# Start, decode and end of a masked-attention kernel on one core: an earlier first load, a split last load, a shorter decode, another order at the end

## The chip, the core and the metric

The kernel runs on one core of a Trainium2 chip, on its five engines: TensorE (PE, matmuls and transposes), VectorE (DVE), ScalarE (ACT), GpSimd (POOL, which issues the loads of the adjacency) and SyncE (SP, which issues the other transfers). The metric is device time in microseconds of one launch. A profiled execution gives the trace that is quoted; its span runs from the first to the last instruction.

## The reference

One layer of graph attention with 4,096 items x and 4,096 entities, followed by a normalisation. The inputs' adjacency is an int32 matrix of 4,096 x 4,096, with a few ones in a row.

```python
scores = (x @ W @ a1)[:, None] + (entity_embs @ W @ a2)[None, :]
e = jnp.where(scores > 0, scores, 0.2 * scores)
e = jnp.where(adj > 0, e, -9e15)
attention = jax.nn.softmax(e, axis=1)
h = attention @ entity_embs + x
x = layernorm(x + elu(h))
```

Write p for the items' scores and q for the entities'. Each weight of the softmax is an exponential of max(p + q, 0.2 (p + q)), where the adjacency has a one.

## The kernel before, in words

The 4,096 items stand in four groups (g) of 1,024 columns, the entities in 32 blocks (b) of 128. A step is one group and one block, 128 in all; two steps are a pair (j), 16 pairs a group. A chunk is four blocks of one group, 32 chunks in all; GpSimd loads each from the int32 adjacency into the bf16 tile `raw` (line 272), which has five buffers, so that load n waits until TensorE has turned chunk n - 5.

**Before the first group.** SyncE loads the weights, the entities (1 MB) and x (four loads). GpSimd waits for the weights (line 280) before its first load. VectorE makes q, p, the scale of the codes and the shift of the softmax (lines 403 to 482) in many small steps; TensorE sends some of them to all partitions.

**Per pair.** TensorE turns it (`turn_pair`, line 698: 16 transposes of 128 x 128 into a PSUM tile `pairs`, of which there are two). ScalarE or VectorE (`by_dve` says which) takes it out as the mask in bf16, scaled (`store_pair`, lines 321 and 523). TensorE adds it to a histogram of codes (`add_hist`, line 714), from which the highest q among an item's neighbours is found.

**Per group, between its histogram and its first step.** ScalarE copies the histogram (line 329), TensorE spreads it (line 729), VectorE decodes it in nine instructions (`decode`, lines 492 to 512) into `dcol`, a column by item: the shift minus the leaky score of p and the highest q. TensorE turns `dcol` into rows over all partitions (`make_row`, line 736) and ScalarE copies them out (`take_row`, line 351, `drow`). For group 0 all this stands between its last chunk and its first step; for the later groups it is laid into the steps of the group before (the constants `HIST_COPY_AT` = 23 to `DROW_AT` = 28 say at which step). In group 0's second half TensorE and ScalarE also make the eight rows of p (`p_row`, lines 673 and 310), one ahead of each pair from pair 8 on; `p_row(c)` on TensorE waits for ScalarE's copy of row c - 1.

**Per step.** VectorE takes the smaller of mask and `drow` for a pair (line 534, `xm`) and adds the larger of p and the bend of q (line 542, `wts`); ScalarE exponentiates (line 335); TensorE sums weighted entities into `acc[0]` (line 749) and the weights into `acc[1]` (line 752). TensorE's steps lag by three.

**The end of a group.** `take_acc` copies both sums on ScalarE, TensorE turns them (`turn_sums`, `turn_back`), and `finish` in eleven parts divides, adds x, applies the elu (its exponential on ScalarE), adds x again, and normalises (the squares on ScalarE, the power on GpSimd). For groups 0 to 2 the parts lie in the steps of the next group (`FINISH_AT`); group 3's stand alone at the end. SyncE stores the result.

The order on each engine is the order of the code; semaphores connect the engines, and an engine does nothing behind an instruction that waits.

Of the kernel before, what the change touches and what calls it, by code (L numbers as in the profile page):

```python
# [5 lines left out]
P = 128  # L6
N, M, F = 4096, 4096, 64
# [11 lines left out]
CHUNKS = STEPS // CHUNK  # L19
RAWS = 5  # L20
# [34 lines left out]
def attention_layernorm(nc, x, adj, ent_blocks, turned_in, weights_in, out):  # L55
# [19 lines left out]
    with ctx:  # L75
# [50 lines left out]
        qbase = sb("qbase", [P, 1], fp32)  # L126
        empty = sb("empty", [P, NT], fp32)
# [26 lines left out]
        adj_in = [sem(f"adj_in{i}") for i in range(RAWS)]  # L154
        x_in = sem("x_in")
# [37 lines left out]
        d_done = sem("d_done")  # L193
        row_mm = sem("row_mm")
# [5 lines left out]
        acc_free = sem("acc_free")  # L200
        turn_sums_mm = sem("turn_sums_mm")
# [44 lines left out]

        def mask_made(engine, j):

            engine.wait_ge(dve_mask_done if by_dve(j) else act_mask_done, sum(by_dve(k) == by_dve(j) for k in range(j + 1)))
# [16 lines left out]
        def _(pool):  # L266
            def load(n):

                g, c = divmod(n, NB // CHUNK)
                if n >= RAWS:  # L270
                    pool.wait_ge(pair_mm, (n - RAWS + 1) * CHUNK // 2)
                pool.dma_start(raw[:, n % RAWS, 0:SIZES[g], :],  # L272
                               rows(adj, g)[:, :, P * CHUNK * c:P * CHUNK * (c + 1)]).then_inc(adj_in[n % RAWS], 16)
# [6 lines left out]
            pool.wait_ge(w_in, 16)  # L280
# [23 lines left out]
        def _(act):  # L304
# [7 lines left out]
            def store_pair(j):  # L312

                i = 2 * j
                if by_dve(j):
                    return
# [4 lines left out]
                act.activation(mask[:, i % RING:i % RING + 2, 0:n], pairs[j % 2][:, :, 0:n], ACT.Relu,  # L321
# [50 lines left out]
            take_row(0)  # L372
# [19 lines left out]
            squares(NG - 1)  # L392

        @block.vector
        def _(dve):
# [26 lines left out]
            def q_scale():  # L422
# [25 lines left out]
                dve.wait_ge(q_step, 6)  # L448
                dve.tensor_scalar(place[:, :], qcol[:, :], qmin_neg[:, :], qinv[:, :], ALU.add, ALU.mult).then_inc(q_step, 1)
# [24 lines left out]
            def find_shift():  # L474
# [7 lines left out]
                dve.tensor_scalar(q_bias[:, :], qcol[:, :], shift[:, :], None, ALU.subtract).then_inc(bias_done, 1)  # L482

            def decode(g):
# [3 lines left out]
                n = 7 * g  # L488
# [12 lines left out]
                dve.tensor_scalar(empty[:, s], st[:, 3, 0:m], 1.0, None, ALU.is_le)  # L501
# [349 lines left out]
```

## Time and profile before

| | |
|---|---|
| median of 3 runs | 354.25 us (353.78 to 355.08) |
| profiled execution | 353.8 us, its span 351.7 us |
| busy in the span | TensorE 80%, VectorE 84%, ScalarE 72%, GpSimd 12% |
| last landing of group 0 used | 52.96 us |
| first mask product (line 534) | 64.29 us |
| last copy out of `acc` begins | 336.91 us |
| last instruction on VectorE begins | 348.60 us |

Three stretches differ. Up to 53 us the engines work between landings of the adjacency; from there to 64 us one chain runs through four engines for group 0's decode; then the steps run to 336 us, and a last chain ends the span. The shares of busy time are means over all of them.

### The profile page before, as it was taken

The numbers are of one execution on the slowest core, as the hardware profiler recorded it, in microseconds if no ns is written. First come the engines' busy times: TensorE is split into PE (matmuls) and PEld (weight loads), VectorE is DVE, ScalarE is ACT, GpSimd is POOL, SyncE is SP. The second block draws the span as 40 slices with busy tenths as digits, with TensorE's granted clock in tenths as the row PEclk, the third lists the DMA queues.
The fourth block names the chain that finished last, engine by engine and source line by source line (L and its number), as shares of the span: only waits on it lengthen the run. The fifth ranks groups of instructions, "written<-read, shape, count | busy, mean of one in ns | idle before, by whom it ended". The sixth has DMA issues, their size and how long they took to land.

```text
span 351.7 us, 7943 instructions
## 1 busy us (share of the span) xinstructions
PE 280.9 (80%) x3470; PEld 142.3 (40%) x3470; DVE 296.7 (84%) x356; ACT 253.6 (72%) x216; POOL 40.9 (12%) x45
## 2 busy tenths in 40 slices
PE   1249675779999989999999999999959696667730
PEld 1146454535445544455445445545423232212210
DVE  1780523799988989999999999999999999999944
ACT  1087563399888949999999899999837764646620
POOL 6011110001101000000000310000040000002201
PEclk9998999699999999999999999999999999999985
DMA  7999999999999968887989591000000000000000
GB/s 149 257 207 208 207 207 207 207 208 206 207 175 187 151 101 126 136 131 120 152 140 145 85 173 32 2 3 2 2 0 32 3 0 2 0 2 0 32 0 30
DMA packets 34817, 37.23 MB, mean 106 GB/s; under 512 B 672, under 2 KB 33504, under 8 KB 34784
## 3 DMA queue, kind: packets, MB, share of 16 engines
q0 software_dynamic: 33280, 33.56, 59.0%
q1 hardware_dynamic: 1504, 3.18, 3.2%
q8 instruction: 27, 0.44, 0.5%
q14 instruction: 6, 0.05, 0.0%
HBM read 69.24 MB, written 1.05 MB: 200 GB/s over the span
## 4 chain that ended last, share of the span: by engine, by line
PE 32%; issue 22%; DVE 21%; DMA 13%; ACT 9%; POOL 2%; POOLq 1%; DVEq 0%; ACTq 0%
PE acc L749 12%; DMA raw<-adj_dram 12%; DVE xm L534 10%; PE pairs L698 10%; PE acc L752 6%; DVE wts L542 5%; ACT mask L321 5%; ACT wts L335 3%; PE hist L714 3%; POOL rstd L278 1%; DVE mask L523 1%; PE misc L729 1%; DMA w_sb<-weights_in_dram 1%; ACT drow L351 1%; POOL raw L272 1%
## 5 line engine op out<-in xcount | busy, mean ns | idle before, releaser
L335 ACT ACTIVATE wts<-wts,q_bias 128x1024 f32<-128x1024 f32 x128 | 143.5, 1150 | 45.1 <-DVE wts L542 44.4
L542 DVE SCALAR_TENSOR_TENSOR wts<-pb,q_bend,xm 128x1024 f32<-128x1024 f32 x128 | 160.5, 1279 | 2.0 <-PE acc L752 1.8
L749 PE MATMUL acc<-wts,ent_sb 128*32 128x512 f32 x1024 | 135.4, 601 | 16.8 <-ACT wts L335 13.1
L321 ACT ACTIVATE mask<-pairs 128x2048 bf16<-128x2048 bf16 x53 | 99.0, 1875 | 28.9 <-PE pairs L698 28.9
L698 PE MATMUL pairs<-ident,raw 128*128 128x128 bf16 x1024 | 71.3, 226 | 13.2 <-DMA raw<-adj_dram 10.3
L534 DVE TENSOR_TENSOR xm<-mask,drow 128x2048 bf16<-128x2048 bf16 x64 | 78.1, 1220 | 2.3 <-ACT drow L351 2.3
L752 PE MATMUL acc<-wts,onesf 128*32 128x256 f32 x1024 | 78.6, 379 | 0.0
L698 PEld LDWEIGHTS pairs<-ident,raw 128*128 128x128 bf16 x1024 | 61.6, 102 | 34.3 <-issue 23.0
L752 PEld LDWEIGHTS acc<-wts,onesf 128*32 128x32 f32 x1024 | 33.1, 111 | 77.6 <-issue 77.6
L272 POOL DMA_DIRECT2D raw<-adj_dram x32 | 28.3, 884 | 173.6 <-PE pairs L698 170.9
L749 PEld LDWEIGHTS acc<-wts,ent_sb 128*32 128x32 f32 x1024 | 26.7, 109 | 42.0 <-ACT wts L335 27.9
L523 DVE TENSOR_SCALAR mask<-pairs 128x2048 bf16<-128x2048 bf16 x11 | 13.5, 1223 | 17.1 <-PE pairs L698 17.1
L278 POOL TENSOR_TENSOR rstd<-var,mhalf 128x8 f32<-128x8 f32 x4 | 11.4, 2859 | 133.5 <-DVE var L612 133.4
L714 PE MATMUL hist<-mask,codes 128*32 128x512 bf16 x256 | 25.6, 395 | 0.8 <-DVE mask L523 0.8
L736 PE MATMUL misc<-ident,dcol 128*128 128x128 bf16 x32 | 3.3, 266 | 8.6 <-DVE dcol L512 8.6
L714 PEld LDWEIGHTS hist<-mask,codes 128*32 128x32 bf16 x256 | 7.0, 96 | 6.9 <-DVE mask L523 1.1
L659 PE MATMUL misc<-identf,qm 128*2 128x128 f32 x2 | 0.6, 394 | 9.6 <-DVE qm L419 9.6
L351 ACT ACTIVATE drow<-misc 128x1024 bf16<-128x1024 bf16 x4 | 4.0, 1010 | 4.9 <-PE misc L736 4.9
L472 DVE TENSOR_REDUCE p_all<-misc 1x1 f32<-1x128 f32 x1 | 0.3, 279 | 8.2 <-PE misc L678 8.2
L736 PEld LDWEIGHTS misc<-ident,dcol 128*128 128x128 bf16 x32 | 2.4, 119 | 10.2 <-DVE dcol L512 10.2
L575 DVE SCALAR_TENSOR_TENSOR y<-ent_sum,empty,misc 128x64 f32<-128x64 f32 x32 | 6.5, 274 | 0.1
L310 ACT ACTIVATE pb<-misc 128x512 f32<-128x512 f32 x8 | 4.8, 595 | 2.4 <-PE misc L673 2.4
(98 smaller groups left out, 101.2 us busy)
## 6 DMA issues: line engine op xcount, KB each, us to landing
raw<-adj_dram POOLq DMA_DIRECT2D x32, 1024.0 KB, 10.5
ent_sb<-ent_blocks_dram SPq DMA_DIRECT2D x1, 1024.0 KB, 7.5
x_sb<-x_dram SPq DMA_DIRECT2D x4, 256.0 KB, 8.6
out_dram<-y SPq DMA_DIRECT2D x4, 256.0 KB, 2.0
w_sb<-weights_in_dram SPq DMA_DIRECT2D x1, 32.5 KB, 2.1
```

The lines of the kernel that those rows point to most:

```text
L272: pool.dma_start(raw[:, n % RAWS, 0:SIZES[g], :], rows(adj, g)[:, :, P * CHUNK * c:P * CHUNK * (c + 1)]).then_inc(adj_in[n % RAWS], 16)
L278: pool.tensor_tensor(rstd[:, 0:n], var[:, 0:n], mhalf[:, 0:n], ALU.pow).then_inc(rstd_done, 1)
L321: act.activation(mask[:, i % RING:i % RING + 2, 0:n], pairs[j % 2][:, :, 0:n], ACT.Relu, scale=2.0 ** LIFT).then_inc(act_mask_done, 1)
L335: act.activation(part, part, ACT.Exp, bias=q_bias[:, b:b + 1]).then_inc(w_done, 1)
L351: act.activation(drow[:, g % 2, 0:cols(g)], row_ps[:, 0:cols(g)], ACT.Copy).then_inc(drow_done, 1)
L523: dve.tensor_scalar(mask[:, i % RING:i % RING + 2, 0:n], pairs[j % 2][:, :, 0:n], 2.0 ** LIFT, 0.0, ALU.mult, ALU.max).then_inc(dve_mask_d ...
L534: dve.tensor_tensor(xm[:, i % XS:i % XS + 2, 0:n], mask[:, i % RING:i % RING + 2, 0:n], drow[:, g % 2, 0:n].unsqueeze(1).to_broadcast([P, ...
L542: dve.scalar_tensor_tensor(wts[:, i % SLOTS, 0:n], pb[:, P * TILE0[g]:P * TILE0[g] + n], q_bend[:, b:b + 1], xm[:, i % XS, 0:n], ALU.max, ...
L698: ins = pe.transpose(pairs[j % 2][:, k, P * t:P * t + P], raw[:, n % RAWS, t, at:at + P], ident[:, :])
L714: ins = pe.matmul(hist[to:to + Q, 0:n], codes[:, i % NB, :], mask[:, i % RING, n * c:n * c + n], start=(pair == 0), stop=(pair == GROUP_PA ...
L749: pe.matmul(acc[0][to:to + Q, 0:n], ent_sb[:, b, Q * f:Q * f + Q], part[:, n * k:n * k + n], start=(b == 0), stop=(b == NB - 1))
L752: ins = pe.matmul(acc[1][Q * k:Q * k + Q, 0:P * m], onesf[:, 0:Q], part[:, P * t:P * t + P * m], start=(b == 0), stop=(b == NB - 1))
```

## The change

1. GpSimd's first load no longer waits for the weights.
2. Chunk 7, the last of group 0 (`LATE`), is loaded as two halves, the second with a semaphore of its own (`late_in`), for which only the last pair of the group waits. That pair's mask is shared: ScalarE takes its first block, VectorE its second; who needs the mask waits for both.
3. The decode has six instructions. Two slopes (`key_slope`) and two bases (`p_base`, `key_base`) are made once in `q_scale` and `find_shift`; the leaky score is then the smaller of two straight lines. `empty` comes last and has a semaphore, for which the totals wait. Group 0's rows are copied out by VectorE.
4. At the end, VectorE copies the last sums of weights while ScalarE copies the features; max(y, 0) + x has a place of its own (in a buffer of `wts`) and no longer waits for the exponential; VectorE squares.

```diff
-            pool.wait_ge(w_in, 16)
             load(0)
@@ load(n)
+                first = CHUNK // 2 if n == LATE else CHUNK
+                pool.dma_start(raw[:, n % RAWS, 0:SIZES[g], 0:P * first],
+                               rows(adj, g)[:, :, P * CHUNK * c:P * (CHUNK * c + first)]).then_inc(adj_in[n % RAWS], 16)
+                if n == LATE:
+                    pool.dma_start(raw[:, n % RAWS, 0:SIZES[g], P * first:P * CHUNK],
+                                   rows(adj, g)[:, :, P * (CHUNK * c + first):P * CHUNK * (c + 1)]).then_inc(late_in, 16)
@@ turn_pair(j)
                 pe.wait_ge(adj_in[n % RAWS], 16 * (n // RAWS + 1))
+                if j == GROUP_PAIRS - 1:
+                    pe.wait_ge(late_in, 16)
@@ who makes a mask
+        def by_act(j):
+            return j == GROUP_PAIRS - 1 or not by_dve(j)
@@ store_pair(j) on ScalarE
+                k = 1 if by_dve(j) else 2
+                act.activation(mask[:, i % RING:i % RING + k, 0:n], pairs[j % 2][:, 0:k, 0:n], ACT.Relu,
...
@@ decode(g), after the reduction
-                dve.tensor_scalar(empty[:, s], st[:, 3, 0:m], 1.0, None, ALU.is_le)
-                dve.tensor_scalar(st[:, 0, 0:m], st[:, 3, 0:m], qstep[:, :], qbase[:, :], ALU.mult, ALU.add).then_inc(st_step, 1)
-                dve.wait_ge(st_step, n + 4)
-                dve.tensor_tensor(st[:, 1, 0:m], st[:, 0, 0:m], pcol[:, s], ALU.add).then_inc(st_step, 1)
+                dve.scalar_tensor_tensor(st[:, 0, 0:m], st[:, 3, 0:m], key_slope[:, 0:1], p_base[:, s], ALU.mult,
+                                         ALU.add).then_inc(st_step, 1)
+                dve.tensor_scalar(st[:, 1, 0:m], st[:, 3, 0:m], key_slope[:, 1:2], key_base[:, :], ALU.mult,
+                                  ALU.add).then_inc(st_step, 1)
                 dve.wait_ge(st_step, n + 5)
-                dve.tensor_scalar(st[:, 2, 0:m], st[:, 1, 0:m], 0.0, 1 - ALPHA, ALU.max, ALU.mult).then_inc(st_step, 1)
-                dve.wait_ge(st_step, n + 6)
-                dve.scalar_tensor_tensor(st[:, 2, 0:m], st[:, 0, 0:m], ALPHA, st[:, 2, 0:m], ALU.mult, ALU.add).then_inc(st_step, 1)
-                dve.wait_ge(st_step, n + 7)
...
-                dve.tensor_scalar(dcol[:, 0:m], st[:, 2, 0:m], -1.0, shift[:, :], ALU.mult, ALU.add).then_inc(d_done, 1)
+                dve.tensor_tensor(dcol[:, 0:m], st[:, 0, 0:m], st[:, 1, 0:m], ALU.min).then_inc(d_done, 1)
+                dve.tensor_scalar(empty[:, s], st[:, 3, 0:m], 1.0, None, ALU.is_le).then_inc(empty_done, 1)
+
+            def take_row(g):
+                dve.wait_ge(row_mm, g + 1)
+                dve.tensor_copy(drow[:, g % 2, 0:cols(g)], row_ps[:, 0:cols(g)]).then_inc(drow_done, 1)
@@ the end, on VectorE (instead of the eleven parts in a row)
+                dve.wait_ge(w_used, STEPS)
...
+                dve.tensor_copy(wsum_sb[0:sums, 0:P * fourth(g)], acc[1][0:sums, 0:P * fourth(g)]).then_inc(last_wsum, 1)
+                for part in range(4):
+                    finish(g, part)
+                dve.wait_ge(att_done, NG)
+                fin_inc(dve.scalar_tensor_tensor(pos, y_g, 0.0, x_gr, ALU.max, ALU.add))
+                fin_wait()
+                dve.wait_ge(elu_done, NG)
+                fin_inc(dve.scalar_tensor_tensor(y_g, e_g, 1.0, pos, ALU.min, ALU.add))
+                for part in (6, 7):
+                    finish(g, part)
+                dve.wait_ge(centred, NG)
+                dve.tensor_tensor(e_g, y_g, y_g, ALU.mult).then_inc(square_done, 1)
+                for part in (8, 9, 10):
+                    finish(g, part)
```

GpSimd's program from its start on, before:

```order
L272 DMA raw<-adj_dram 128x8x512 [waits w_in]
L282 ISA
L282 IOTA steps_k 128x32
L284 MEMSET ident 128x128
L285 MEMSET identf 128x128
L287 AFFINE_SELECT identf<-identf 128x128 [waits ident_done]
L289 AFFINE_SELECT ident<-ident 128x128
L272 DMA raw<-adj_dram 128x8x512 x4
L272 DMA raw<-adj_dram 128x8x512 [waits pair_mm] x26
```

The same place on GpSimd in the changed kernel:

```order
L288 DMA raw<-adj_dram 128x8x512
L300 ISA
L300 IOTA steps_k 128x32
L302 MEMSET ident 128x128
L303 MEMSET identf 128x128
L305 AFFINE_SELECT identf<-identf 128x128 [waits ident_done]
L307 AFFINE_SELECT ident<-ident 128x128
L288 DMA raw<-adj_dram 128x8x512 x4
L288 DMA raw<-adj_dram 128x8x512 [waits pair_mm] x2
L288 DMA raw<-adj_dram 128x8x256 [waits pair_mm]
L291 DMA raw<-adj_dram 128x8x256
L288 DMA raw<-adj_dram 128x8x512 [waits pair_mm] x23
```

The first load has lost its wait; what stands behind it moves up with it, and the eighth load is now two of half the width.

VectorE at the end of group 0 before, from its own masks of that group (line 523) to the first mask product (line 534):

```order
L523 TENSOR_SCALAR mask<-pairs 128x2048 [waits pair_mm] x4
L492 SCALAR_TENSOR_TENSOR above<-misc,steps_key 128x256 [waits spread_mm]
L495 SCALAR_TENSOR_TENSOR above<-misc,above 128x256 [waits st_step]
L498 TENSOR_REDUCE st<-above 128x4x2 [waits st_step]
L501 TENSOR_SCALAR empty<-st 128x8 [waits st_step]
L502 TENSOR_SCALAR st<-st,qstep,qbase 128x8
L504 TENSOR_TENSOR st<-st,pcol 128x8 [waits st_step]
L506 TENSOR_SCALAR st<-st 128x8 [waits st_step]
L508 SCALAR_TENSOR_TENSOR st<-st 128x8 [waits st_step]
L512 TENSOR_SCALAR dcol<-st,shift 128x8 [waits st_step]
L534 TENSOR_TENSOR xm<-mask,drow 128x2048 [waits drow_done,act_mask_done,p_rows]
```

The same place on VectorE in the changed kernel:

```order
L553 TENSOR_SCALAR mask<-pairs 128x2048 [waits pair_mm] x3
L553 TENSOR_SCALAR mask<-pairs 128x1024 [waits pair_mm]
L518 SCALAR_TENSOR_TENSOR above<-misc,steps_key 128x256 [waits spread_mm]
L521 SCALAR_TENSOR_TENSOR above<-misc,above 128x256 [waits st_step]
L524 TENSOR_REDUCE st<-above 128x4x2 [waits st_step]
L529 SCALAR_TENSOR_TENSOR st<-st,key_slope,p_base 128x8 [waits shift_step,st_step]
L531 TENSOR_SCALAR st<-st,key_slope,key_base 128x8
L536 TENSOR_TENSOR dcol<-st 128x8 [waits st_step]
L537 TENSOR_SCALAR empty<-st 128x8
L541 COPY drow<-misc 128x1024 [waits row_mm]
L564 TENSOR_TENSOR xm<-mask,drow 128x2048 [waits drow_done,act_mask_done,p_rows]
```

The fourth mask is half as wide, the three steps that each waited for the one ahead have gone, `empty` stands behind `dcol`, and the copy of the rows has come over from ScalarE.

VectorE in the tail before, from the totals (line 560) to the variance (line 609):

```order
L560 SCALAR_TENSOR_TENSOR total<-empty,hist 128x8 [waits turn_sums_mm]
L565 RECIPROCAL total<-total 128x8 [waits sums_taken]
L575 SCALAR_TENSOR_TENSOR y<-ent_sum,empty,misc 128x64 [waits out_done,sum_done,turn_back_mm]
L590 TENSOR_TENSOR y<-y,total 128x512 [waits fin_step,feats_taken]
L593 TENSOR_TENSOR y<-y,x_sb 128x512 [waits fin_step]
L597 SCALAR_TENSOR_TENSOR y<-y,x_sb 128x512 [waits elu_done,att_done]
L600 SCALAR_TENSOR_TENSOR y<-e,y 128x512 [waits fin_step]
L603 TENSOR_REDUCE mean<-y 128x8 [waits fin_step]
L606 SCALAR_TENSOR_TENSOR y<-mean,y 128x512 [waits fin_step]
L609 TENSOR_REDUCE var<-e 128x8 [waits square_done]
```

The same place on VectorE in the changed kernel:

```order
L658 COPY wsum_sb<-acc 128x256 [waits turn_sums_mm,w_used]
L591 SCALAR_TENSOR_TENSOR total<-empty,hist 128x8 [waits empty_done,turn_sums_mm]
L596 RECIPROCAL total<-total 128x8 [waits sums_taken]
L606 SCALAR_TENSOR_TENSOR y<-ent_sum,empty,misc 128x64 [waits out_done,sum_done,turn_back_mm]
L621 TENSOR_TENSOR y<-y,total 128x512 [waits fin_step,feats_taken]
L624 TENSOR_TENSOR y<-y,x_sb 128x512 [waits fin_step]
L662 SCALAR_TENSOR_TENSOR wts<-y,x_sb 128x512 [waits att_done]
L665 SCALAR_TENSOR_TENSOR y<-e,wts 128x512 [waits elu_done,fin_step]
L634 TENSOR_REDUCE mean<-y 128x8 [waits fin_step]
L637 SCALAR_TENSOR_TENSOR y<-mean,y 128x512 [waits fin_step]
L669 TENSOR_TENSOR e<-y 128x512 [waits centred]
L640 TENSOR_REDUCE var<-e 128x8 [waits square_done]
```

A copy and the squares have come to VectorE, and the wait for the exponential stands one instruction later.

## Rows read from the trace of the kernel before

**Rows 1.** The chain that ended last, in order of time: start us, us, what.

```profile
31.22 21.70 DMA raw<-adj_dram
```

**Rows 2.** Waits of TensorE's line 698 up to 60 us: releaser, us, times.

```profile
  DMA raw<-adj_dram: 10.3, 8
```

**Rows 3.** Stretches: us, busy us of engines (instructions), clock, DMA share, GB/s.

```profile
70.00:160.00 90.00, 86.50 (x1144) 44.53 (x1148) 84.65 (x83) 79.63 (x65) 10.52 (x12) 1.00 1.02 164
210.00:330.00 120.00, 99.86 (x1188) 41.14 (x1188) 118.76 (x135) 88.18 (x80) 7.50 (x2) 0.99 0.04 8
```

**Rows 4.** DMA queues, 3.5 to 7 us: packets, MB, share of 16 engines.

```profile
q1 hardware_dynamic: 202, 0.83, 102.2%
```

**Rows 5.** DMA queues, 10 to 15 us.

```profile
q0 software_dynamic: 495, 0.51, 59.4%
q1 hardware_dynamic: 493, 0.91, 54.7%
```

**Rows 6.** DMA queues, 16 to 53 us.

```profile
q0 software_dynamic: 7570, 7.64, 124.0%
```

**Rows 7.** Timeline, 3 to 9 us: start us, us, instruction [idle before it, releaser].

```profile
3.13 1.03 POOL L272 DMA_DIRECT2D raw<-adj_dram  x1 [2.68 <-DMA w_sb<-weights_in_dram]
...
4.62 0.29 DVE L406 COPY wa_row<-acc 128x128 f32<-128x128 f32 x1 [1.27 <-PE acc L653]
...
8.93 2.29 DVE L411 TENSOR_TENSOR wts<-ent_sb,wa_row 128x2048 f32<-128x2048 f32 x1 [4.02 <-DMA ent_sb<-ent_blocks_dram]
```

**Rows 8.** Timeline, 47.5 to 58 us, the end of group 0.

```profile
51.51 0.62 PE L673 MATMUL misc<-identf,pcol 128*128 128x128 f32 x4 [0.41 <-ACT pb L310]
52.17 0.60 ACT L310 ACTIVATE pb<-misc 128x512 f32<-128x512 f32 x1 [0.80 <-PE misc L673]
...
52.96 1.07 PE L698 MATMUL pairs<-ident,raw 128*128 128x128 bf16 x16 [0.83 <-DMA raw<-adj_dram]
...
54.06 1.88 ACT L321 ACTIVATE mask<-pairs 128x2048 bf16<-128x2048 bf16 x1 [1.30 <-PE pairs L698]
...
55.87 1.23 DVE L523 TENSOR_SCALAR mask<-pairs 128x2048 bf16<-128x2048 bf16 x1 [3.84 <-PE pairs L698]
...
57.15 0.40 PE L714 MATMUL hist<-mask,codes 128*32 128x512 bf16 x4 [0.76 <-DVE mask L523]
```

**Rows 9.** Timeline, 126 to 130 us, group 1's decode.

```profile
126.92 0.42 DVE L498 TENSOR_REDUCE st<-above 128x8 f32<-128x256 f32 x1
...
127.37 0.17 DVE L501 TENSOR_SCALAR empty<-st 128x8 f32<-128x8 f32 x1
127.45 0.28 DVE L502 TENSOR_SCALAR st<-st,qstep,qbase 128x8 f32<-128x8 f32 x1
...
128.38 0.23 DVE L512 TENSOR_SCALAR dcol<-st,shift 128x8 bf16<-128x8 f32 x1
128.52 2.47 DVE L542 SCALAR_TENSOR_TENSOR wts<-pb,q_bend,xm 128x1024 f32<-128x1024 f32 x2
...
128.67 0.62 PE L736 MATMUL misc<-ident,dcol 128*128 128x128 bf16 x8 [0.91 <-DVE dcol L512]
```

**Rows 10.** Timeline, 62 to 66 us, group 0's rows.

```profile
63.14 1.02 ACT L351 ACTIVATE drow<-misc 128x1024 bf16<-128x1024 bf16 x1 [4.94 <-PE misc L736]
...
64.29 1.22 DVE L534 TENSOR_TENSOR xm<-mask,drow 128x2048 bf16<-128x2048 bf16 x1 [2.29 <-ACT drow L351]
```

**Rows 11.** Timeline, 315 to 352 us, the tail.

```profile
336.91 0.38 ACT L360 ACTIVATE wsum_sb<-acc 128x256 f32<-128x256 f32 x1
...
337.34 0.61 PE L767 MATMUL hist<-identf,wsum_sb 128*128 128x4 f32 x4 [0.99 <-ACT wsum_sb L360]
...
341.59 0.63 ACT L340 ACTIVATE e<-y 128x512 f32<-128x512 f32 x1 [4.30 <-DVE y L593]
...
342.32 0.69 DVE L597 SCALAR_TENSOR_TENSOR y<-y,x_sb 128x512 f32<-128x512 f32 x1 [0.77 <-ACT e L340]
343.05 0.69 DVE L600 SCALAR_TENSOR_TENSOR y<-e,y 128x512 f32<-128x512 f32 x1
```

More of the change, by code:

```diff
@@ L126, in attention_layernorm @@
         qbase = sb("qbase", [P, 1], fp32)
+        key_slope = sb("key_slope", [P, 2], fp32)
+        key_base = sb("key_base", [P, 1], fp32)
+        base_diff = sb("base_diff", [P, 1], fp32)
+        p_base = sb("p_base", [P, NT], fp32)
         empty = sb("empty", [P, NT], fp32)
@@ L245, in by_dve @@
             return g == 0 and k >= 9 and k % 2 == 1 or g == 1 and k % 3 == 2 or g == 2 and k in (2, 5)
+        def by_act(j):
+            return j == GROUP_PAIRS - 1 or not by_dve(j)
         def mask_made(engine, j):
-            engine.wait_ge(dve_mask_done if by_dve(j) else act_mask_done, sum(by_dve(k) == by_dve(j) for k in range(j + 1)))
+            if by_act(j):
+                engine.wait_ge(act_mask_done, sum(by_act(k) for k in range(j + 1)))
+            if by_dve(j):
+                engine.wait_ge(dve_mask_done, sum(by_dve(k) for k in range(j + 1)))
         @block.sync
@@ L314, in store_pair @@
                 i = 2 * j
-                if by_dve(j):
+                if not by_act(j):
                     return
@@ L482, in find_shift @@
                 dve.tensor_scalar(q_bias[:, :], qcol[:, :], shift[:, :], None, ALU.subtract).then_inc(bias_done, 1)
+                dve.tensor_tensor(base_diff[:, :], shift[:, :], qbase[:, :], ALU.subtract).then_inc(shift_step, 1)
+                dve.scalar_tensor_tensor(key_base[:, :], qbase[:, :], -ALPHA, shift[:, :], ALU.mult, ALU.add).then_inc(shift_step, 1)
+                dve.wait_ge(shift_step, 5)
+                dve.tensor_scalar(p_base[:, :], pcol[:, :], ALPHA - 1, base_diff[:, :], ALU.mult, ALU.add).then_inc(shift_step, 1)
             def decode(g):
@@ L522, in store_pair @@
                 n = cols(i // NB)
-                dve.tensor_scalar(mask[:, i % RING:i % RING + 2, 0:n], pairs[j % 2][:, :, 0:n], 2.0 ** LIFT, 0.0, ALU.mult,
-                                  ALU.max).then_inc(dve_mask_done, 1)
+                k = 1 if by_act(j) else 0
+                dve.tensor_scalar(mask[:, i % RING + k:i % RING + 2, 0:n], pairs[j % 2][:, k:2, 0:n], 2.0 ** LIFT, 0.0,
+                                  ALU.mult, ALU.max).then_inc(dve_mask_done, 1)
             def masked(j):
@@ L617, in finish, with finish_last @@
                         y_done if g + 1 < NG else last_done, 1)
+            def finish_last():
+                g = NG - 1
+                n, sums = SIZES[g], Q * len(fourths(g))
+                y_g, e_g, x_gr = y[:, 0:n, :], e[:, 0:n, :], x_sb[:, TILE0[g]:TILE0[g] + n, :]
+                pos = wts[:, 0, 0:n * F].rearrange("p (t f) -> p t f", f=F)
+                dve.wait_ge(w_used, STEPS)
+                dve.wait_ge(turn_sums_mm, g)
+                dve.tensor_copy(wsum_sb[0:sums, 0:P * fourth(g)], acc[1][0:sums, 0:P * fourth(g)]).then_inc(last_wsum, 1)
[12 more added lines that the diff above has]
+                    finish(g, part)
             q_columns()
@@ L644, in _ @@
                         masked(s // 2 + 1)
-            for part in range(11):
-                finish(NG - 1, part)
+            finish_last()
         @block.tensor
```

30 lines of the change are left out of this document (20 added, 10 removed).

## The prediction, made before the changed kernel was run

> **What bounds the kernel now.** I read the chain of waits first, since the change touches the start, the four decodes and the end, and only what lies on the path pays. In its first 53 us the chain is loads of the adjacency: its longest piece is a load of 21.70 us that ends where the transposes of the first group's last chunk begin [rows 1]. TensorE stood idle 10.3 us in eight waits, one for each chunk of that group, before line 698 [rows 2]. So the first 53 us are set by the DMA. The DMA packets by queue say how full it is: the adjacency's queue alone uses 124.0% of sixteen engines (packets overlap) from 16 to 53 us [rows 6]. Then, from the windows by engine, TensorE is busy 86.50 of 90 us between 70 and 160, and VectorE 118.76 of 120 us between 210 and 330 [rows 3]. These two stages have no slack and no load to wait for: a microsecond won before them arrives later as a microsecond, and a microsecond taken out of VectorE there is won as well. Last, the timelines of the first group's end, of a decode and of the tail give the terms.
>
> **Part 1: loads at once.** The first load is issued at 3.13 us, after 2.68 us of waiting for the weights [rows 7]; the other engines begin at 0.74, so the issue moves up by 2.4 us. What that is worth at 53 us depends on whether the DMA engines are idle meanwhile. From 3.5 to 7 us the hardware queue (the load of the entities) is the only one that moves anything, at 102.2% [rows 4]; between 10 and 15 us that queue and the adjacency's share the engines, 54.7 and 59.4% [rows 5]. So most of what the earlier load moves, it moves in place of the entities. Ends: nothing (the engines were full), and the whole 2.4 us (they were free). I take 0.5 us, near the first: the entities alone reach 102.2% where two queues reach 114 and the adjacency 124, and 12 to 20% of 3.5 us is 0.4 to 0.7.
> The Trainium skill (DMA: Bandwidth & Descriptors, "Issuing engines are not separate DMA queues") says that DMAs issued by different engines run on the same sixteen DMA engines and interleave, so that an earlier issue from another engine saves the issue's own time only. By that rule the term is nearly 0 and the sum below 0.5 us smaller; the trace agrees as far as the entities' queue fills the engines alone.
> The entities land later for it. VectorE starts on them at 8.93 [rows 7], and TensorE's first transposes stand behind what it makes of them. That is covered: the 10.3 us of idle time in [rows 2] are the room by which TensorE may be late.
>
> **Part 2: the last chunk.** The chunk lands at 52.96, where TensorE had idled 0.83 us only [rows 8]. So half a chunk that lands some 2.5 us earlier (half of a load: 7,570 packets in 37 us and 1,040 a load, so 5.1 us [rows 6]) can be used 0.83 us and a bit earlier, not 2.5: before it TensorE is held by the transposes of the scores at 51.51, which waited for ScalarE's copy. Followed through: pair 14 is turned at 52.0 (51.51 + 0.62, less the overlap of 0.1) to 53.07; ScalarE takes its mask (1.88) from 53.1 and the last score row (0.60) from 54.9, and is free at 55.45; pair 15 needs the second half by 53.85, and gets it at 52.96; ScalarE's half of its mask, 128x1024 out of PSUM, takes the 1.02 of the same shape in [rows 10], so the last histogram starts at 56.45, against 57.15 [rows 8]. That is 0.7 us. VectorE's half (half of 1.23) is done long before; ScalarE is what ends last. The price of smaller packets (512 bytes written instead of 1,024) is hidden up to 0.9 us, since the second half may land as late as 53.85. No row shows such packets: the bounds are half the present time each (no loss) and the whole present time each (the chunk takes 5 us more, a rival below). I take the first with a small surcharge, hidden.
>
> **Part 3: the decode.** Nine instructions become six; the first three stay. From the end of the reduction (126.92 + 0.42) to the end of dcol (128.38 + 0.23) stand 1.27 us, and to VectorE's next instruction 1.15 us after line 501's start [rows 9]. The new chain has two steps instead of five: two independent instructions, the second with two column operands as line 502 (0.28, starting 0.1 to 0.14 behind), then the minimum (0.17 as line 501, with 0.04 between dependent ones): 0.63 to dcol. "empty" follows and costs 0.08. So 0.6 earlier for who waits for dcol, 0.5 for VectorE itself. Group 0: on the path, 0.6. Group 1: TensorE idled 0.91 for dcol [rows 9] and is the bound after, 0.6. Groups 2 and 3: VectorE is the bound, 0.5 each. In all 2.2 us. The three new instructions of the shift and the two slopes lie in the first 36 us, where VectorE waits for loads: nothing.
> In group 0 the row is copied by VectorE instead of ScalarE. Now: copy at 63.14, mask product at 64.29, 1.15 us [rows 10]. The nearest row for the new copy is line 523 (out of PSUM, bf16, 1.23 for 2,048 elements), so 0.6 for 1,024 and 0.05 to the next: 0.45 won. From the other side, the fp32 copy of line 406 (0.29 for 128 [rows 7]) would make it as slow as ScalarE's or slower: down to -0.1. I go by line 523, whose type it has.
>
> **Part 4: the end.** The sums are copied by VectorE while ScalarE copies the features: ScalarE's second copy began at 336.91 and released TensorE at 337.34 [rows 11]. VectorE can begin where ScalarE's first did, at 336.4, and takes between 0.29 (line 406, 128 elements) and twice that for 256; I take 0.42: 336.89, so 0.45 won, and the features' copy is done at 337.0, before the transposes that need it. Then max(y, 0) + x: now it starts at 342.32, behind ScalarE's exponential (341.59, 0.63), and is followed by line 600 at 343.05 [rows 11]. It moves beside the exponential and line 600 starts at 342.32: 0.73 won. The squares go from ScalarE (0.63 for this shape) to VectorE (0.69 as its neighbours): 0.07 lost. In all 1.1 us.
>
> **The sum.** 0.5 + 0.7 + 2.2 + 0.45 + 1.1 = 4.95, say 5.0 us. The profiled execution took 353.8 (span 351.7 and 2.1 around it): 348.8. The median of the runs is 0.45 above it, so 349.2.
>
> **Rivals.**
> A. The DMA engines had room: the first load's 2.4 us arrive whole. For it: 102% is below the 124% that the same engines reach later. Against: no packet of the adjacency is seen from 3.5 to 7 us. 1.9 us less: 347.3.
> B. The later decodes don't pay (1.6 us): the next thing that VectorE waits for, a ScalarE exponential or a freed buffer, is late instead. For: ScalarE works right behind VectorE all along. Against: [rows 3], VectorE has 1.2 idle us in 120. 350.8.
> C. Packets of 512 bytes take as long as those of 1,024. The second half lands 5 us later, at 57.5, and the last histogram starts 1.07 + 1.02 + 0.1 later, 59.7, against the forecast's 55.95: 3.8 us more, 353.0. It decides from a surcharge of 0.9 us on.
> The Trainium skill (DMA: Bandwidth & Descriptors, "Specifications") puts the smallest transfer at line rate at 512 bytes; by it C is off, just. No run here shows it.
> D. Slower: the early load and its four followers, now issued before the entities are through, are served first. Five loads of 5.1 us from 3 us on and then the entities (1.05 MB at the 0.83 MB in 3.5 us of [rows 4], 4.4 us): these land near 32 instead of 8.9, 23 us late; the room of some 8 to 10 us is used up, and 14 us stay: about 363. It decides where the entities land after 18 us. For: a queue that comes first can hold the engines alone, as the entities' does in [rows 4]. Against: in [rows 5] the two queues share evenly.
> E. The chain has another end that I don't see, so that nothing moves: 354.
>
> **How the numbers follow.** Forecast 0.61, A 0.13, B 0.13, C 0.06, D 0.04, E 0.03. The forecast's own range is 348.2 to 350.4 (first load 0 to 1, decode and copies half a microsecond either way). For 8 in 10 I take in A and B with their own spread: 347.0 to 351.6. No change is within 0.5% (1.8 us) of 354.25, what a measurement of this kernel can tell: C and E, 0.09; slower is D, 0.04; faster is the rest, 0.87.
>
> **What would show it.** Last histogram of group 0 at 55.9 instead of 57.15 (first load 0.5, split 0.7); from there to the first mask product 6.1 us instead of 7.1. If the DMA packets of the second half end after 54 us, C is at work. If VectorE starts on the entities after 10.5, part 1 has been paid by them, and after 18 D is true. The first chunk should be turned at about the same time as now. Decode, from the end of the reduction to VectorE's next exponent: 0.65 instead of 1.15. Tail, from the last matmul of line 752 to the end: 1.1 us shorter. I am wrong if the whole of the first load's 2.4 us is found at the last chunk's landing, or if the span from the first mask product to VectorE's last exponent shortens by much less than 1.6 us.

## The result and the profile after

The changed kernel takes 348.83 us (median of 4 runs, 348.58 to 350.18) against 354.01 us before on the same chip (353.51 to 355.08): a ratio of 0.9859, 95% interval 0.983 to 0.9889. Predicted were 349.2 us, 347.0 to 351.6. The profiled execution has a span of 347.1 us instead of 351.7.

From landmark to landmark of the two traces the 4.66 us between the last instructions on VectorE (348.60 and 343.94) divide like this, in us:

| stretch | before | after | won | predicted |
|---|---|---|---|---|
| to the turning of the seventh chunk | 47.89 | 47.66 | 0.23 | 0.5 |
| from there to the last histogram of group 0 | 9.26 | 8.50 | 0.76 | 0.7 |
| from there to the first mask product | 7.14 | 6.20 | 0.94 | 0.6 + 0.45 |
| from there to ScalarE's first copy of the tail | 272.12 | 270.51 | 1.61 | 1.6 |
| from there to VectorE's last instruction | 12.19 | 11.07 | 1.12 | 1.1 |

**The first load.** The waits of TensorE for the chunks of group 0 (releaser, us, times; see [rows 2]):

```profile
  DMA raw<-adj_dram: 6.6, 6
```

The DMA queues of the changed kernel from 3.5 to 7 us (packets, MB, share of 16 engines; see [rows 4]):

```profile
q1 hardware_dynamic: 196, 0.80, 97.8%
q0 software_dynamic: 22, 0.02, 3.8%
```

And from the timelines from 1 to 10 us, the first load's issue and VectorE's start on the entities (see [rows 7]):

```profile
1.24 1.03 POOL L288 DMA_DIRECT2D raw<-adj_dram  x1 [0.79 <-POOLq L902]
...
9.04 2.29 DVE L431 TENSOR_TENSOR wts<-ent_sb,wa_row 128x2048 f32<-128x2048 f32 x1 [3.93 <-DMA ent_sb<-ent_blocks_dram]
```

The issue moved up by 1.9 us, not by the 2.4 that I had counted, and bought 22 of the 1,040 packets of a load. VectorE's start on the entities moved by 0.1 us only, so rival D is out.

**The end of group 0.** The timeline of the changed kernel from 47.5 to 58 us (see [rows 8]):

```profile
51.27 0.62 PE L727 MATMUL misc<-identf,pcol 128*128 128x128 f32 x4 [0.41 <-ACT pb L328]
51.73 1.06 PE L754 MATMUL pairs<-ident,raw 128*128 128x128 bf16 x16
...
52.82 1.88 ACT L340 ACTIVATE mask<-pairs 128x2048 bf16<-128x2048 bf16 x1 [0.30 <-PE pairs L754]
...
53.53 1.06 PE L754 MATMUL pairs<-ident,raw 128*128 128x128 bf16 x16
...
54.60 0.59 ACT L328 ACTIVATE pb<-misc 128x512 f32<-128x512 f32 x1
54.63 0.69 DVE L553 TENSOR_SCALAR mask<-pairs 128x1024 bf16<-128x1024 bf16 x1 [2.84 <-PE pairs L754]
...
55.07 1.03 ACT L340 ACTIVATE mask<-pairs 128x1024 bf16<-128x1024 bf16 x1
56.16 0.40 PE L770 MATMUL hist<-mask,codes 128*32 128x512 bf16 x4 [1.00 <-ACT mask L340]
```

Neither half of the chunk is waited for any more: both turnings follow the instruction ahead of them on TensorE. ScalarE has no gap from 52.82 to 56.10, and the last histogram waits for it. VectorE's half was done at 55.32.

**A decode.** Group 1's, on VectorE and TensorE, 124 to 127.5 us (see [rows 9]):

```profile
124.98 0.42 DVE L524 TENSOR_REDUCE st<-above 128x8 f32<-128x256 f32 x1
125.44 0.23 DVE L529 SCALAR_TENSOR_TENSOR st<-st,key_slope,p_base 128x8 f32<-128x8 f32 x1
125.58 0.28 DVE L531 TENSOR_SCALAR st<-st,key_slope,key_base 128x8 f32<-128x8 f32 x1
125.90 0.17 DVE L536 TENSOR_TENSOR dcol<-st 128x8 bf16<-128x8 f32 x1
125.98 0.16 DVE L537 TENSOR_SCALAR empty<-st 128x8 f32<-128x8 f32 x1
126.06 2.47 DVE L572 SCALAR_TENSOR_TENSOR wts<-pb,q_bend,xm 128x1024 f32<-128x1024 f32 x2
...
126.12 0.62 PE L792 MATMUL misc<-ident,dcol 128*128 128x128 bf16 x8 [0.29 <-DVE dcol L536]
```

From the end of the reduction to the end of `dcol` it takes 0.67 us instead of 1.27, and from the start of the instruction behind the reduction to VectorE's next exponent 0.62 instead of 1.15. TensorE's idle time before the rows fell from 0.91 to 0.29.

**Group 0's rows**, on VectorE, timeline 60 to 64 us (see [rows 10]):

```profile
61.53 0.69 DVE L541 COPY drow<-misc 128x1024 bf16<-128x1024 bf16 x1 [1.05 <-PE misc L792]
62.36 1.23 DVE L564 TENSOR_TENSOR xm<-mask,drow 128x2048 bf16<-128x2048 bf16 x1
```

From the start of the copy to the mask product it takes 0.83 us instead of 1.15.

**The tail**, timeline from 315 us on (see [rows 11]):

```profile
332.87 0.42 DVE L658 COPY wsum_sb<-acc 128x256 f32<-128x256 f32 x1 [2.90 <-PE acc L808]
...
333.35 0.61 PE L824 MATMUL hist<-identf,wsum_sb 128*128 128x4 f32 x4 [0.55 <-DVE wsum_sb L658]
...
337.60 0.63 ACT L359 ACTIVATE e<-y 128x512 f32<-128x512 f32 x1 [4.13 <-DVE y L624]
337.60 0.69 DVE L662 SCALAR_TENSOR_TENSOR wts<-y,x_sb 128x512 f32<-128x512 f32 x1
338.34 0.69 DVE L665 SCALAR_TENSOR_TENSOR y<-e,wts 128x512 f32<-128x512 f32 x1
...
340.51 0.69 DVE L669 TENSOR_TENSOR e<-y 128x512 f32<-128x512 f32 x1
```

The exponential and line 662 start together, and line 665 follows the former's start by 0.74 us; before, its counterpart followed by 1.46.

### The profile page after: what moved, and what is told of

It is laid out like the page before. It is cut to its first block, busy times and chain, and to the rows that moved or that the text cites. A ratio compares the mean times of both kernels' runs of the same rounds, so it can differ in the third digit from the quotient of the medians.

```text
span 347.1 us, 7951 instructions
## 1 busy us (share of the span) xinstructions
PE 284.2 (82%) x3470; PEld 145.0 (42%) x3470; DVE 296.9 (86%) x356; ACT 252.4 (73%) x214; POOL 41.9 (12%) x46
## 4 chain that ended last, share of the span: by engine, by line
PE 32%; issue 22%; DVE 20%; DMA 12%; ACT 11%; POOL 2%; POOLq 1%; DVEq 0%; ACTq 0%
PE acc L805 12%; DMA raw<-adj_dram 12%; PE pairs L754 10%; DVE xm L564 10%; ACT mask L340 6%; PE acc L808 6%; DVE wts L572 5%; ACT wts L354 3%; PE hist L770 2%; POOL rstd L297 1%; PE misc L785 1%; DVE y L631 1%; DVE var L640 1%; DVE above L521 1%; DVE st L524 0%
## 5 line engine op out<-in xcount | busy, mean ns | idle before, releaser
L805 PE MATMUL acc<-wts,ent_sb 128*32 128x512 f32 x1024 | 136.9, 607 | 15.4 <-ACT wts L354 11.6
L340 ACT ACTIVATE mask<-pairs 128x2048 bf16<-128x2048 bf16 (+1 forms) x54 | 100.0, 1860 | 27.8 <-PE pairs L754 27.8
L754 PE MATMUL pairs<-ident,raw 128*128 128x128 bf16 x1024 | 73.1, 229 | 9.6 <-DMA raw<-adj_dram 6.6
L808 PE MATMUL acc<-wts,onesf 128*32 128x256 f32 x1024 | 80.1, 385 | 0.0
L754 PEld LDWEIGHTS pairs<-ident,raw 128*128 128x128 bf16 x1024 | 63.3, 103 | 30.7 <-issue 22.9
L805 PEld LDWEIGHTS acc<-wts,ent_sb 128*32 128x32 f32 x1024 | 27.5, 110 | 40.2 <-ACT wts L354 25.3
L553 DVE TENSOR_SCALAR mask<-pairs 128x2048 bf16<-128x2048 bf16 (+1 forms) x11 | 12.9, 1173 | 15.2 <-PE pairs L754 15.1
L727 PE MATMUL misc<-identf,pcol 128*128 128x128 f32 x32 | 5.1, 282 | 1.4 <-ACT pb L328 1.2
L431 DVE TENSOR_TENSOR wts<-ent_sb,wa_row 128x2048 f32<-128x2048 f32 x1 | 2.3, 2291 | 3.9 <-DMA ent_sb<-ent_blocks_dram 3.9
```

Of the source, the lines that this page charges most:

```text
L340: act.activation(mask[:, i % RING:i % RING + k, 0:n], pairs[j % 2][:, 0:k, 0:n], ACT.Relu, scale=2.0 ** LIFT).then_inc(act_mask_done, 1)
L553: dve.tensor_scalar(mask[:, i % RING + k:i % RING + 2, 0:n], pairs[j % 2][:, k:2, 0:n], 2.0 ** LIFT, 0.0, ALU.mult, ALU.max).then_inc(dve_ ...
L754: ins = pe.transpose(pairs[j % 2][:, k, P * t:P * t + P], raw[:, n % RAWS, t, at:at + P], ident[:, :])
L805: pe.matmul(acc[0][to:to + Q, 0:n], ent_sb[:, b, Q * f:Q * f + Q], part[:, n * k:n * k + n], start=(b == 0), stop=(b == NB - 1))
L808: ins = pe.matmul(acc[1][Q * k:Q * k + Q, 0:P * m], onesf[:, 0:Q], part[:, P * t:P * t + P * m], start=(b == 0), stop=(b == NB - 1))
```

## The experiments

The theory that the runs test: the first 53 us are set by the DMA engines' work, the end of group 0 by ScalarE, the rest by chains with no slack, so that each part's gain is local and arrives whole. The rivals are those of the prediction. Where small terms are at stake the landmarks of the trace are compared, since whole times scatter by more (see e9). Kernels e1 and e3 to e7 ran once each.

**e1: the wait for the weights is back.**

```diff
+            pool.wait_ge(w_in, 16)
             load(0)
```

> The changed kernel with the wait for the weights put back ahead of the first load, nothing else. Theory: the entities' packets hold the DMA engines until about 7.5 us, so the earlier issue bought next to nothing: the first load is issued near 3.1 instead of 1.24 us, and the chunks still land where they do in the changed kernel (second chunk turned at 21.4, seventh at 47.7, each within 0.3 us); last histogram of group 0 at 56.2 to 56.4; span 347.1 to 347.4. The prediction's own size (0.5 us): last histogram at 56.7, span 347.6. Rival A (the issue counts whole, 1.9 us): seventh chunk at 49.5, last histogram at 58, span 349.

Measured: issue at 3.06, seventh chunk turned at 48.07 instead of 47.66, last histogram at 56.57 instead of 56.16, both 0.41 us later, between the 0.3 at most of the theory and the 0.5 of the prediction. The seventh chunk's first transposes in the changed kernel, then in e1:

```profile
47.66 1.07 PE L754 MATMUL pairs<-ident,raw 128*128 128x128 bf16 x16 [0.82 <-DMA raw<-adj_dram]
```

```profile
48.07 1.07 PE L755 MATMUL pairs<-ident,raw 128*128 128x128 bf16 x16 [0.98 <-DMA raw<-adj_dram]
```

The seven traces without the wait and with the changed kernel's loads ahead of that chunk (its own twice) have it between 47.55 and 47.77; the two with it, 47.89 and 48.07. So the early issue is worth about 0.3 us, and rival A, by which all of its 1.9 us would arrive, is out. The span of 348.6 is 1.1 us longer than this accounts for; where that comes from is e9's.

**e2: the entities gapless.** `ent_flat` is a view of four mask buffers that are free until pair 20; VectorE's first product reads the entities from there.

```diff
-            sp.dma_start(ent_sb[:, :, 0:F], ent_blocks).then_inc(ent_in, 16)
+            sp.dma_start(ent_flat, ent_blocks).then_inc(ent_in, 16)
...
+            act.wait_ge(ent_in, 16)
+            act.activation(ent_sb[:, :, 0:F], ent_flat, ACT.Copy).then_inc(ent_spread, 1)
```

> The changed kernel, but the entities are loaded into a gapless tile (8 KB runs per partition instead of 256 bytes with a gap of 4) and ScalarE spreads them into their place; same bytes. Theory: what the first load waits for is engine time that the entities' short runs take (1 MB in 4.4 us, 238 GB/s); in long runs they take 2.6 to 3.1 us, and every chunk lands 1.3 to 1.8 us earlier: the seventh is turned at about 46.1, the last histogram of group 0 stands at about 54.6, span about 345.6. Rival: the first adjacency load has a fixed latency of 4 to 5 us of its own, or the engines were not full, so that the chunks land where they did (47.7) and the span stays at 347.1; VectorE would still start on the entities 1 to 2 us earlier.

Measured: 348.2 us (347.03 to 349.08, ratio 0.9833, 0.9792 to 0.9873), profiled span 346.4. VectorE starts on the entities at 6.51 instead of 9.04, the seventh chunk is turned at 45.84 instead of 47.66 and the last histogram stands at 54.34, the last two 1.82 us earlier. The turning, and the DMA queues of this kernel from 3.5 to 7 us:

```profile
45.84 1.07 PE L760 MATMUL pairs<-ident,raw 128*128 128x128 bf16 x16 [0.81 <-DMA raw<-adj_dram]
```

```profile
q1 hardware_dynamic: 199, 1.06, 76.7%
q0 software_dynamic: 138, 0.14, 23.9%
```

The hardware queue (the entities and, from about 6 us on, the first of x) moves 1.06 MB in place of 0.80 in the same stretch, in 76.7% of the engines, and the adjacency has the rest. So the engines were full of the entities' short runs, and this work, more than the issue, stood ahead of the adjacency. The theory's upper end is met. Whether the short runs or the gaps between them cost the time was not separated.

The rival's latency exists, but did not set the landings. The adjacency's first packet comes 4.2 us after its issue in the kernel before (7.29 us) and in the changed one (5.43), and 4.6 us in e2 (5.87). Later in the kernel, with the queues idle, a load needs 1.6 us for it (issue at 130.48 and first packet at 132.06 in the kernel before); why the first needs more is not shown. In the changed kernel few packets follow until the entities' last at 8.3 us; in e2 the entities end at 6.1, just behind the first packet. That a still shorter load of the entities would meet this latency is likely, but was not tried.

In the span 1.2 of the 1.8 us are lost again later, as in e1.

**e3: the last mask whole on VectorE.**

```diff
-            return j == GROUP_PAIRS - 1 or not by_dve(j)
+            return not by_dve(j)
```

> The changed kernel with the mask of the first group's last pair made by VectorE alone, as before the change (the split load stays). Theory: ScalarE is what ends last there, since it still has the mask of pair 14 and the last row of scores to do (free at 55.07), and VectorE stands ready at 54.63: VectorE alone needs 1.22 us, ends at 55.85, last histogram at 55.9 instead of 56.16, so the sharing costs 0.25 us; span 346.9. Rival (the sharing is what shortens the end): ScalarE and VectorE in parallel halve the time, so undoing it makes the histogram 0.5 us later, 56.7, span 347.6.

Measured: span 346.8. VectorE's mask and the last histogram of this kernel:

```profile
54.70 1.23 DVE L553 TENSOR_SCALAR mask<-pairs 128x2048 bf16<-128x2048 bf16 x1 [2.84 <-PE pairs L754]
55.98 0.40 PE L770 MATMUL hist<-mask,codes 128*32 128x512 bf16 x4 [0.76 <-DVE mask L553]
```

55.98 instead of 56.16, with the turnings 0.07 later: the sharing costs 0.25 us. It puts half of the last mask on the engine that is late. That the span fits the expected 346.9 is luck: it holds 0.41 us less between the histogram and the mask product (see e9) and 0.37 more in the tail, where VectorE's last instruction waits 2.19 us for GpSimd instead of 1.82; no run explains the latter.

**e4: the last chunk in one load.**

```diff
-                first = CHUNK // 2 if n == LATE else CHUNK
+                first = CHUNK
```

The second load and its wait are left out as well.

> The changed kernel with the first group's last chunk as one load again (the shared mask stays). Theory: pair 14 begins with the whole landing, 52.7 to 52.95 instead of 51.73, and ScalarE, which carries the chain from there, is late by the same: last histogram at 57.15 to 57.4 instead of 56.16, span 348.1 to 348.3; the split is worth 1.0 to 1.2 us with ScalarE in the chain. Rival: the split does nothing or costs (the smaller packets are as dear as the larger): histogram at 56.2 or earlier, span 347.1 or less.

Measured: pair 14 turned at 52.67, last histogram at 57.11, 0.95 us later than in the changed kernel.

```profile
52.67 1.07 PE L749 MATMUL pairs<-ident,raw 128*128 128x128 bf16 x16 [0.82 <-DMA raw<-adj_dram]
...
57.11 0.40 PE L765 MATMUL hist<-mask,codes 128*32 128x512 bf16 x4 [1.01 <-ACT mask L337]
```

So the split is what won there, and the sharing took a part of it back. The kernel before, with neither, says the same: from the seventh chunk to the last histogram it takes 9.25 us, and e4, with the sharing alone, 9.49. The span, 349.8, holds 1.8 us more than that: 0.6 between histogram and mask product and 1.2 after, both as in e9.

**e5: all chunks of group 0 in halves.**

```diff
+                width = CHUNK // 2 if n <= LATE else CHUNK
+                for at in range(0, CHUNK, width):
+                    pool.dma_start(raw[:, n % RAWS, 0:SIZES[g], P * at:P * (at + width)],
```

> The changed kernel with all eight chunks of the first group loaded as two halves each (packets of 512 bytes written instead of 1,024); a chunk is turned when both have landed, the last as in the changed kernel. It measures the price of the smaller packets by itself, seven times over. Theory: the changed kernel's two halves moved 0.79 MB in the 4 us from 47 to 51, 5% slower than the 207 GB/s of whole loads, so a chunk costs 0.25 us more and the seventh chunk is turned 1.5 to 1.8 us later, at 49.2 to 49.5; last histogram near 57.8, span near 348.8. Rival C (each packet costs what a large one does): 5 us for each chunk, the seventh turned near 82, span above 380. No price at all: 47.7 and 347.1.

Measured: seventh chunk turned at 49.70, last histogram at 58.20, both 2.04 us later and a little above what was expected; span 349.1. The turning in e5, and the DMA from 20 to 40 us in the changed kernel and in e5:

```profile
49.70 1.07 PE L753 MATMUL pairs<-ident,raw 128*128 128x128 bf16 x16 [1.11 <-DMA raw<-adj_dram]
```

```profile
DMA packets 4093, 4.14 MB, mean 207 GB/s; under 512 B 61, under 2 KB 4092, under 8 KB 4092
```

```profile
DMA packets 7809, 3.95 MB, mean 198 GB/s; under 512 B 122, under 2 KB 7808, under 8 KB 7808
```

Over seven chunks that is 0.29 us each, and in the steady stream 198 GB/s instead of 207: packets of 512 bytes cost 5 to 6% more for the same bytes. Rival C's 5 us a chunk are out.

**e6: nine instructions in the later decodes.** The lines of before are put back for g of 1 to 3.

```diff
+                if g == 0:
...
+                dve.tensor_scalar(st[:, 2, 0:m], st[:, 1, 0:m], 0.0, 1 - ALPHA, ALU.max, ALU.mult).then_inc(st_step, 1)
+                dve.wait_ge(st_step, n + 6)
+                dve.scalar_tensor_tensor(st[:, 2, 0:m], st[:, 0, 0:m], ALPHA, st[:, 2, 0:m], ALU.mult, ALU.add).then_inc(st_step, 1)
```

> The changed kernel with the decode of groups 1 to 3 in nine instructions as before (group 0 keeps six). Theory: each is a stretch of VectorE's own path, 0.5 us, and all three arrive at the end: the distance from the first mask product of group 0 to the last matmul grows by 1.5 to 1.6 us, span 348.6 to 348.7. Rival B (what VectorE wins it waits for elsewhere): the distance stays within 0.3 us, span 347.1 to 347.4.

Measured: 272.06 us from the first mask product to the tail instead of 270.51, 1.55 us more; pair by pair it comes in three jumps of 0.51 to 0.52 us, at the mask products of pairs 15, 31 and 47, the first behind each decode. Rival B is out. The span, 349.0, holds 0.37 us more in the tail, where VectorE's line 675 starts that much later behind the exponential; no run explains it.

**e7: the last row of scores on VectorE.**

```diff
+                if j == GROUP_PAIRS - 1:
+                    dve.wait_ge(p_mm, ROWS)
+                    dve.tensor_scalar(pb[:, N - 512:N], misc[:, :], 1 - ALPHA, None, ALU.mult).then_inc(p_rows, 1)
                 store_pair(j)
```

ScalarE leaves this row out.

> The changed kernel with the last row of scores taken out of PSUM by VectorE, idle there, instead of ScalarE. Theory: ScalarE carries the end of group 0; without the row's 0.5 us it starts its half of the last mask at 54.6 instead of 55.07 and ends at 55.65: last histogram at 55.7 instead of 56.16, span 346.65. Rival (the transposes or the landing set the end, ScalarE only seems to): the histogram stays at 56.1 to 56.2, span 347.1.

Measured: last histogram at 55.59, 0.57 us earlier, 0.11 of it because the turnings were; span 346.1, of which 0.41 us is the shorter way from the histogram to the mask product that e9 explains. ScalarE's two masks now follow each other, and the histogram still waits for them:

```profile
52.71 2.83 ACT L340 ACTIVATE mask<-pairs 128x2048 bf16<-128x2048 bf16 x2 [0.30 <-PE pairs L757]
...
53.62 0.69 DVE L683 TENSOR_SCALAR pb<-misc 128x512 f32<-128x512 f32 x1 [1.94 <-PE misc L730]
...
55.59 0.40 PE L773 MATMUL hist<-mask,codes 128*32 128x512 bf16 x4 [0.55 <-ACT mask L340]
```

**e8: e2 and e7 together, and the last squares on ScalarE.**

> The changed kernel with three edits: the entities loaded gapless and spread by ScalarE, the last row of scores taken by VectorE, and the last squares on ScalarE again. Theory: 1.3 to 1.8 us, 0.45 us and 0.07 us add up, since the first moves all landings and the second shortens what follows the last: span 344.8 to 345.3, median 346.5 to 347. Rival (the entities' run length does not matter): span 346.6, median 348.3. If ScalarE's copy of the entities or an earlier landing runs into another bound, the sum is less than its parts and shows at the last histogram, expected at 54.1.

Measured: 346.71 us (346.37 to 348.16), ratio 0.9815 (0.9789 to 0.9842); span 344.9, last histogram at 54.08, tail 11.01. The parts add up. Two of five executions are 1.0 and 1.5 us longer.

**e9: spare work for TensorE.** Open by then: e1, e2 and e4 have 1.1 to 1.2 us more between the first mask product and the tail than the other kernels with six instructions, and all of it lies between the mask products of pairs 5 and 7. From the histogram to the mask product these kernels take 5.79, 6.20 or 6.78 us with the same instructions.

```diff
+            def keep_busy(to, count):
+                for _ in range(count):
+                    pe.matmul(to[:, 0:P], ident[:, :], ident[:, :], start=True, stop=True)
```

> The changed kernel with 72 spare matmuls of 128x128 on TensorE, whose products nobody reads, where it waits after group 0: 8 before the spread, 24 before the rows, 10 behind them and 30 before pair 18. Open after the other runs: equal kernels differ by 1.1 to 1.2 us, all of it between the sixth and the eighth mask product after group 0 (three runs of the ones before have it, five not), and by 0.4 us between the last histogram and the first mask product. Theory: TensorE's granted clock falls to half after its idle time, once near 58 us always, and in some executions again near 71, where TensorE is the bound. Kept busy it stays at 1.0: last histogram to first mask product 5.6 to 5.8 us instead of 6.2, no execution with the later loss, span 346.5 to 346.7, times within 0.5 us of each other. Rival (the differences are not the clock's, or the spare matmuls only make TensorE late): that distance grows to 6.5 or more, span 347.4 or more, and the times scatter by 1.2 us as before.

The spare matmuls stand in TensorE's waits at the end of group 0 and ahead of pair 18. Measured: 348.57 us, all four executions between 348.46 and 348.72; span 346.8; histogram to mask product 5.79. Stretches of the changed kernel, of e1 and of e9 (columns as in [rows 3]; the granted clock is the third from the end). The changed kernel:

```profile
58.00:62.00 4.00, 1.40 (x12) 0.99 (x11) 2.41 (x8) 0.00 (x0) 0.00 (x0) 0.62 1.24 207
...
70.00:74.00 4.00, 3.34 (x48) 2.22 (x48) 4.00 (x4) 4.00 (x5) 0.00 (x0) 1.00 1.24 207
```

e1, with the wait back:

```profile
58.00:62.00 4.00, 1.81 (x15) 1.40 (x14) 2.00 (x8) 0.00 (x0) 0.00 (x0) 0.78 1.24 206
...
70.00:74.00 4.00, 3.26 (x24) 2.02 (x28) 4.00 (x4) 4.00 (x4) 0.00 (x0) 0.57 1.24 207
```

e9, with the spare matmuls:

```profile
58.00:62.00 4.00, 2.99 (x47) 2.64 (x45) 2.64 (x8) 0.00 (x0) 0.00 (x0) 1.00 1.25 208
...
70.00:74.00 4.00, 3.65 (x52) 2.38 (x56) 4.00 (x5) 4.00 (x4) 0.00 (x0) 1.00 1.24 207
```

The clock falls to 1.2 GHz in the first stretch in the changed kernel and in e1, not in e9. e1's falls a second time at 70 to 74 us, and it gets 24 matmuls done there where the changed kernel gets 48. That is its 1.1 us, and with TensorE the bound from there on it is never made up. The rows of e2 and e4 show the same second fall (0.57 from 68 to 72 and from 72 to 76 us). The spare matmuls take both falls away. A low clock between the mask product and that place costs nothing: in e5 the first fall lasts until 70.5 us (0.50 from 62 to 70), and its steps take 270.48 us.

The first fall explains the three distances. On TensorE two groups of instructions stand between the histogram and the mask product, and what counts is which of them meet it. In the changed kernel (6.20), the spreading is done at full clock and the rows at half:

```profile
57.26 1.10 PE L785 MATMUL misc<-stack,acc_sb 128*128 128x64 f32 x8 [0.70 <-ACT acc_sb L348]
...
60.47 1.03 PE L792 MATMUL misc<-ident,dcol 128*128 128x128 bf16 x8 [2.10 <-DVE dcol L536]
```

In e4 (6.78) both are slow:

```profile
58.21 1.68 PE L780 MATMUL misc<-stack,acc_sb 128*128 128x64 f32 x8 [0.70 <-ACT acc_sb L345]
...
61.99 1.04 PE L787 MATMUL misc<-ident,dcol 128*128 128x128 bf16 x8 [2.10 <-DVE dcol L533]
```

In e9 (5.79) neither is, and in e3 and e7 (5.79) the clock falls only behind the rows; this is e9's row:

```profile
60.57 0.62 PE L792 MATMUL misc<-ident,dcol 128*128 128x128 bf16 x8 [0.76 <-DVE dcol L536]
```

The differences, 0.41 and 0.58 us, are those of the distances. The kernel before met the fall as the changed one did (1.10 and 1.04 us), so that the comparison of the two is fair.

**e10: e8 and the spare matmuls; e11: the changed kernel again,** on the same chip as e9.

> The changed kernel with the entities gapless, the last row of scores on VectorE, the last squares on ScalarE, and the 72 spare matmuls. Theory: the clock's 0.4 us come on top of the other three edits and the scatter goes: span 344.4 to 344.6, median 346.2, all executions within 0.6 us. Rival (the spare matmuls cost what they save): span 344.9 or more and times up to 348 as without them.

> The changed kernel itself, unaltered, beside the two others on the same chip. Both theories: median 348.6 to 349.2, with one or two of five executions 1.1 to 1.5 us longer; its profile with the later fall of the clock has the span at 348.2, without it at 347.1.

Measured: e10 346.18 us, all four executions between 346.15 and 346.39, ratio 0.9779 (0.9759 to 0.9799), span 344.3. e11 349.96 us (six executions: three from 348.89 to 349.29, three from 350.62 to 350.96), ratio 0.9884 (0.986 to 0.9908); its profile, at 347.1, is one without the second fall. Its median misses the expected 348.6 to 349.2, since three of six are long. So e10 is the fastest version, 3.8 us faster than the changed kernel on that chip by the medians; 2.8 us by the spans of two executions without the second fall.

## Why the prediction was right, point by point

**First load: mechanism right, term too large.** I had 0.5 us, from the 12 to 20% by which the entities alone seemed to leave the engines idle. The runs give 0.23 (profile against profile) to 0.41 (e1), about 0.3. The engines were nearly full, 97.8% by the entities' queue. The measured term lies between my 0.5 and the near 0 of the Trainium skill's rule (DMA: Bandwidth & Descriptors, "Issuing engines are not separate DMA queues"). e2 shows what does help: less work for the sixteen engines, 1.8 us of it. One sign I read too simply: that no packet of the adjacency was seen from 3.5 to 7 us need not mean that the entities kept it out, since its first packet comes 4.2 us or more after the issue in each trace.

**Last chunk: right to 0.1 us**, because it was followed through TensorE's and ScalarE's queues instead of crediting half a landing (2.5 us). 0.76 measured. Two things I priced only together: the split is worth 0.95 (e4), the sharing -0.25 (e3). That ScalarE ends last was in the text; that the sharing therefore costs was not drawn from it. The smaller packets, which no row had shown, cost 0.29 us a chunk (e5), under the 0.9 that were hidden.

**Decode: right.** 0.60 for who waits for `dcol`, 0.53 for VectorE, against 0.6 and 0.5; the three later ones give 1.61 between the two profiles and 1.55 in e6, against 1.6. Between the two profiles each of the three brings 0.53 to 0.54 by the first mask product behind it, group 1's too: the 0.6 that I gave it on TensorE's side is not seen. The sum fits since I had rounded the other two down to 0.5.

**Rows of group 0: 0.32 instead of 0.45.** The copy took 0.69 rather than 0.6, and 0.14 passed to the mask product rather than 0.05.

**Tail: right.** 0.45 + 0.72 - 0.07 is 1.10 by the starts of lines 824, 665 and 640 against their predecessors, and 1.12 between the landmarks.

**The sum: 5.0 predicted, 4.6 in the span**: the first load and the rows are 0.4 short, the rest 0.1 over. That the profiled time, 348.85 us, meets my 348.8 all the same is luck: what lies around the span shrank from 2.1 to 1.8 us, for which I had no term. The medians moved by 5.2 us. Whole times of this kernel are the worse measure: in the changed kernel (with e11) and e8, six of fifteen executions (three of six in e11) are 1.3 to 2.1 us longer than the shortest of their kernel. In the traces of e1, e2 and e4 such a loss is a second fall of TensorE's clock. That it is the cause in the executions without a trace is inferred from e9 and e10, where both the fall and the scatter are gone in eight of eight. Their mean clock does not settle it: the three long ones of e11 have 0.944 to 0.950 against 0.952 to 0.958, but those of e8 have no lower clock than its others. I had no case for it.

## What to carry to other kernels

While one queue keeps the DMA engines full, an earlier issue on another queue moves little; look instead at what the full queue spends its time on, above all short runs with gaps. To price an earlier landing or a shared instruction, walk through every engine's queue up to the next join: sharing work with the engine that is late there costs time. Small dependent instructions on the path of the bounding engine are worth their whole length.

## What the runs showed of the hardware

- Loading 1 MB into runs of 256 bytes with gaps of 4 held the loads behind it back by 1.8 us more than loading it into runs of 8 KB (e2).
- Casting loads with 512 bytes written per packet cost 0.29 us more per MB than with 1,024, and ran at 198 GB/s instead of 207 (e5).
- The first packet of the first casting load came 4.2 to 5.0 us after its issue in the thirteen traces. Later, with the queue idle, it took 1.6 us (issue at 130.48 us, first packet at 132.06, in the kernel before).
- TensorE's granted clock fell to half at the end of group 0 in each of the eleven traces without spare work; the eight transposes of the rows took 1.03 us instead of 0.62 where they met the fall. In e1, e2 and e4 it fell again, 10 to 14 us after the first fall, and the steps took 1.1 to 1.2 us more. With 72 spare matmuls in the idle time it stayed at 1.00 there (from 54 to 78 us in e9 and e10), and the executions agreed within 0.3 us instead of 2 (e9, e10, e11).
